# Layer norm, attention and routed experts on one core: a mask product per score group, a projection slot by slot, and an output stage cut into pieces of 14, 14 and 4 tiles

## The reference

```python
xn = layernorm(x)
qkv = xn @ W_qkv                       # 32 query heads, 16 key and value heads, of 64
scores = q k^T / 8 + slope[h] * (key position - query position), causal
s = (softmax(scores) v) @ W_out
# experts: 8, each 128 -> 512 -> 128 with gelu, two per token, weights from a softmax over the two
g = silu(experts(xn))
return x + s * g
```

## Time and profile before

| | |
|---|---|
| median of three executions | 1264.25 us |
| profiled execution | 1263.92 us |
| its span | 1262.0 us |
| TensorE busy | 1154.3 us, 91% of the span, 17610 products |
| VectorE busy | 1015.8 us, 80% |
| ScalarE busy | 935.5 us, 74% |
| GpSimd busy | 879.9 us, 70% |
| GpSimd, L743 (low parts) | 640 times 1038 ns |
| VectorE, L1348 (accumulation) | 64 times, mean 687 ns in the loops |
| TensorE, L881 (128 columns) | 1024 times, mean 219 ns |

### The profile page before, as it was taken

How to read it: one execution, slowest core, us unless ns; L and a number is a source line. 1 busy time by engine, 2 the same in 40 slices (tenths; PEclk the granted TensorE clock), 3 DMA queues, 4 the chain that set the end, 5 groups by cost and what they waited for, 6 DMA issues and landing times.

```text
span 1262.0 us, 54043 instructions
## 1 busy us (share of the span) xinstructions
PE 1154.3 (91%) x17610; PEld 915.0 (73%) x17610; DVE 1015.8 (80%) x3107; ACT 935.5 (74%) x1790; POOL 879.9 (70%) x1088
## 2 busy tenths in 40 slices
PE   1449999999999999998999789999999999999992
PEld 0327777777777777787888658777777777777782
DVE  8758888888888888885777668888888888888874
ACT  1328888888888888886666468888888888888882
POOL 9128888888888888884000068888888888888883
PEclk9669999999999999999999989999999999999996
DMA  6416666666666666674333366665555555555553
GB/s 211 171 38 134 142 140 148 143 142 144 144 142 144 144 142 144 145 141 93 86 89 82 99 156 137 136 137 133 133 133 133 133 133 133 133 133 133 133 116 84
DMA packets 286165, 165.10 MB, mean 131 GB/s; under 512 B 175011, under 2 KB 274691, under 8 KB 285445
## 3 DMA queue, kind: packets, MB, share of 16 engines
q1 hardware_dynamic: 281988, 155.63, 53.9%
q0 software_dynamic: 4096, 8.40, 2.3%
HBM read 15.76 MB, written 16.78 MB: 26 GB/s over the span
## 4 chain that ended last, share of the span: by engine, by line
PE 78%; DVE 6%; DMA 4%; issue 4%; ACT 3%; SPq 2%; POOL 2%; ACTq 0%; POOLq 0%; DVEq 0%
PE ps L880 10%; PE ps L854 10%; PE ps L782 8%; PE ps L783 7%; PE ps L784 7%; PE ps L884 6%; PE outs L911 6%; PE outs L915 5%; PE outs L913 5%; PE ps L881 4%; DMA k_st<-stage 3%; PE ps L887 2%; PE ps L863 2%; ACT q_st L1109 2%; PE outs L783 1%
## 5 line engine op out<-in xcount | busy, mean ns | idle before, releaser
L743 POOL TENSOR_TENSOR t_lo<-stage 128x512 f16<-128x512 f32 x640 | 654.6, 1038 | 106.6 <-ACT stage L1120 102.1
L1302 DVE CUSTOM_DVE_ANT_0 stage<-ps,kmask 128x512 bf16<-128x512 f32 (+3 forms) x1024 | 467.1, 488 | 118.8 <-PE ps L854 101.6
L1120 ACT ACTIVATE stage<-ps,slope 128x512 f32<-128x512 f32 (+1 forms) x768 | 455.6, 619 | 120.0 <-PE ps L887 82.1
L880 PE MATMUL ps<-q_st,k_st 128*128 128x256 f16 (+3 forms) x1024 | 305.8, 301 | 10.5 <-ACT stage L1120 6.9
L911 PE MATMUL outs<-v_sp,stage 128*128 128x65 f16 x2560 | 282.1, 194 | 4.3 <-DVE stage L1332 2.8
L913 PE MATMUL outs<-v_sp,stage 128*128 128x64 f16 x2560 | 281.9, 193 | 0.0
L915 PE MATMUL outs<-v_sp,t_lo 128*128 128x65 f16 x2560 | 281.8, 193 | 0.0
L854 PE MATMUL ps<-k_st,stage 128*128 128x512 f16 (+3 forms) x1024 | 251.7, 302 | 12.8 <-DVE spread L1302 5.5
L911 PEld LDWEIGHTS outs<-v_sp,stage 128*128 128x128 bf16 x2560 | 238.4, 98 | 12.2 <-issue 4.4
L913 PEld LDWEIGHTS outs<-v_sp,stage 128*128 128x128 bf16 x2560 | 235.9, 98 | 9.0 <-issue 0.3
L915 PEld LDWEIGHTS outs<-v_sp,t_lo 128*128 128x128 f16 x2560 | 235.9, 98 | 0.0
(11 more groups left out here) (199 smaller groups left out, 2731.6 us busy)
## 6 DMA issues: line engine op xcount, KB each, us to landing
k_st<-stage SPq DMA_DIRECT2D x256, 128.0 KB, 2.5
q_st<-stage SPq DMA_DIRECT2D x256, 128.0 KB, 2.4
q_st<-stage SPq DMA_DIRECT2D x256, 64.0 KB, 2.1
k_st<-stage SPq DMA_DIRECT2D x128, 64.0 KB, 2.1
slot_y<-stage SPq DMA_DIRECT2D x40, 128.0 KB, 2.0
X<-in_L_attn_inputs SPq DMA_DIRECT2D x8, 512.0 KB, 6.3
slot_x<-att SPq DMA_DIRECT2D x2, 2048.0 KB, 8.7
wx_raw<-in_L_ffn_w SPq DMA_DIRECT2D x64, 64.0 KB, 1.8
```

The lines of the kernel that those rows point to most:

```text
L743: pool.tensor_tensor(t_lo[r], t_p[r], upper(t_p[r]), ALU.subtract).then_inc(s[f"lo{u % NG}"], 1)
L880: pe.matmul(d, k[:, 0, at], q[:, 0, seen], start=True, stop=False, skip_group_check=True)
L1120: e = act.activation(t_p[r][:, c0:c1], S_ps[u % 2][:, c0:c1], ACT.Exp, scale=slope[:, bass.ds(pair_index(n) * 2 * SLOTS + sl * 2 + h, 1)])
L1302: ins = dve.tensor_tensor_reduce(junk[h][:, c0:c0 + w], M_ps[h][:, c0:c0 + w], kmask[:, SEQ - w:SEQ], -1.0 / 1024, 3e38, ALU.add, ALU.min, ...
```

## The change

1. `scores`: the mask product is made once per group, after all blocks, with an output in two pieces (67 columns in each block) where the group has two, and `late_q` read twice by a broadcast. The first product of the second block no longer has the start flag.
2. `project`: the wait for the bank comes first; then for each slot a wait for its transpose and the three products of all four token tiles.
3. `accumulate` multiplies by 1/WS, 64 times, in place of the factor in the output stage.
4. The output goes in pieces of 14, 14 and 4 tiles (1792, 1792 and 512 columns), a multiplication and an addition each: piece 0 on GpSimd, piece 1 on VectorE ahead of its last accumulation, piece 2 on VectorE after it. ScalarE applies Silu to pieces 0 and 1 ahead of the last cast of the last body (`out_hi` of body 63, slot 1), and to piece 2 after it. Pieces 0 and 1 wait for the accumulations of the first 56 bodies.

The expert stage is the same in both kernels.

```diff
+        LAST = NT - QT
+        PIECES = [(0, LAST // 2), (LAST // 2, LAST), (LAST, NT)]
+
         def out_chunk(v, c):
-            return v[:, 8 * c:8 * c + 8, :].rearrange("p t d -> p (t d)")
+            t0, t1 = PIECES[c]
+            return v[:, t0:t1, :].rearrange("p t d -> p (t d)")
+
+        def finish(eng, c):
+            need(eng, "silu", c + 1)
+            eng.wait_ge(s["acc"], BODIES if c == 2 else BODIES - PAIRS)
+            eng.wait_ge(s["xend"], 64)
+            a, g, xx = (out_chunk(v, c) for v in (att, mix, X))
+            eng.tensor_tensor(a, a, g, ALU.mult).then_inc(s[f"gated{c}"], 1)
+            eng.wait_ge(s[f"gated{c}"], 1)
+            eng.tensor_tensor(xx, xx, a, ALU.add).then_inc(s[f"fin{c}"], 1)
...
@@ sync
-            for c, name in ((0, "finP"), (2, "finD"), (1, "finP"), (3, "finD")):
-                sp.wait_ge(s[name], c % 2 + 1)
-                sp.dma_start(ot[:, 8 * c:8 * c + 8, :], X[:, 8 * c:8 * c + 8, :]).then_inc(s["outd"], 16)
+            for c, (t0, t1) in enumerate(PIECES):
+                sp.wait_ge(s[f"fin{c}"], 1)
+                sp.dma_start(ot[:, t0:t1, :], X[:, t0:t1, :]).then_inc(s["outd"], 16)
...
@@ gpsimd, after leave_bodies
-            pool.wait_ge(s["xend"], 64)
-            for c in range(2):
-                pool.wait_ge(s["gated"], c + 1)
-                xx = out_chunk(X, c)
-                pool.tensor_tensor(xx, xx, out_chunk(att, c), ALU.add).then_inc(s["finP"], 1)
+            finish(pool, 0)
...
@@ tensor, scores
-                    pe.matmul(d, k[:, 0, at], q[:, 0, seen], start=True, stop=False, skip_group_check=True)
+                    pe.matmul(d, k[:, 0, at], q[:, 0, seen], start=(c0 == 0), stop=False, skip_group_check=True)
...
-                    late = slice(0, P - LATE - 1)
-                    mm = pe.matmul(d[:, LATE:P], late_k[late, :], late_q[late, LATE:P],
-                                   start=False, stop=True, skip_group_check=True)
-                mm.then_inc(s[f"scored{u % NG}"], 1)
+                late, first = slice(0, P - LATE - 1), [c0 // P for _, _, c0 in GROUPS[u % NG]]
+                d = S_ps[u % 2].rearrange("p (t c) -> p t c", c=P)[:, first[0]:first[-1] + 1:max(first[-1], 1), LATE:P]
+                pe.matmul(d, late_k[late, :], late_q[late, LATE:P].unsqueeze(1).to_broadcast([P - LATE - 1, len(first), P - LATE]),
+                          start=False, stop=True, skip_group_check=True).then_inc(s[f"scored{u % NG}"], 1)
@@ tensor, project
+                bank_free(n, "O0")
                 for sl in range(SLOTS):
                     need(pe, f"ta{sl}", (n + 1) * 16)
-                bank_free(n, "O0")
-                for t in range(QT):
-                    tok = slice(t * P, (t + 1) * P)
-                    for sl in range(SLOTS):
-                        j = bass.ds(pair_index(n) * SLOTS + sl, 1)
+                    j = bass.ds(pair_index(n) * SLOTS + sl, 1)
+                    for t in range(QT):
+                        tok = slice(t * P, (t + 1) * P)
                         mm = three(bank_of("O0")[:, tok], aT[par][sl][:, tok],
...
-                                   start=(sl == 0), stop=(sl == SLOTS - 1))
+                                   start=(sl == 0 and t == 0), stop=(sl == SLOTS - 1), shared_bank=True)
                 mm.then_inc(s["op"], 1)
@@ scalar
+            def gates(c):
+                g = out_chunk(mix, c)
+                act.activation(g, g, ACT.Silu).then_inc(s["silu"], 1)
+
             def out_hi(n, _, sl):
+                final = isinstance(n, int) and (n, sl) == (BODIES - 1, 1)
+                if final:
+                    act.wait_ge(s["added"], NT)
+                    for c in range(2):
+                        gates(c)
                 act.wait_ge(s[f"nrm{sl}"], n + 1)
...
                 act.copy(by_head(a16[sl][:, 0:SEQ]), values_of(sl)).then_inc(s[f"ah{sl}"], 1)
+                if final:
+                    gates(2)
...
-            act.wait_ge(s["added"], NT)
-            act.activation(mix[:, :, :], mix[:, :, :], ACT.Silu).then_inc(s["silu"], 1)
@@ vector
             def accumulate(n, _par, _):
+                if isinstance(n, int) and n == BODIES - 1:
+                    finish(dve, 1)
                 dve.wait_ge(s["op"], n + 1)
...
-                dve.tensor_tensor(a, bank_of("O0")[:, :], a, ALU.add).then_inc(s["acc"], 1)
+                dve.scalar_tensor_tensor(out=a, in0=bank_of("O0")[:, :], scalar=1.0 / WS, in1=a, op0=ALU.mult,
+                                         op1=ALU.add).then_inc(s["acc"], 1)
...
-            dve.wait_ge(s["silu"], 1)
-            dve.wait_ge(s["acc"], BODIES)
-            dve.wait_ge(s["xend"], 64)
-            for c in range(4):
-                a, g, xx = (out_chunk(v, c) for v in (att, mix, X))
-                dve.scalar_tensor_tensor(out=a, in0=a, scalar=1.0 / WS, in1=g, op0=ALU.mult, op1=ALU.mult)\
-                   .then_inc(s["gated"], 1)
-                if c >= 2:
-                    dve.wait_ge(s["gated"], c + 1)
-                    dve.tensor_tensor(xx, xx, a, ALU.add).then_inc(s["finD"], 1)
+            finish(dve, 2)
```

More of the change, by code:

```diff
@@ L277, in build @@
             xload0 xload1 hmm0 hmm1 gelu0 gelu1 hhi hlo0 hlo1 ymm yout ystore0 ystore1
-            gated rd0 rd1 nrm0 nrm1 op acc ta0 ta1 ah0 ah1 al0 al1 rows
+            gated0 gated1 gated2 rd0 rd1 nrm0 nrm1 op acc ta0 ta1 ah0 ah1 al0 al1 rows
             turnc0 turnc1 crow0 crow1 copied
@@ L281, in build @@
             qmm0 qmm1 qh0 qh1 ql0 ql1 kmm kh kl vmm vh vl
-            finD finP outd""".split()
+            fin0 fin1 fin2 outd""".split()
         s = {n: sem("s_" + n) for n in names}
@@ L597, in _ @@
             ot = out.rearrange("b (t p) d -> p (b t) d", p=P)
-            for c, name in ((0, "finP"), (2, "finD"), (1, "finP"), (3, "finD")):
-                sp.wait_ge(s[name], c % 2 + 1)
-                sp.dma_start(ot[:, 8 * c:8 * c + 8, :], X[:, 8 * c:8 * c + 8, :]).then_inc(s["outd"], 16)
-            sp.wait_ge(s["outd"], 64)
+            for c, (t0, t1) in enumerate(PIECES):
+                sp.wait_ge(s[f"fin{c}"], 1)
+                sp.dma_start(ot[:, t0:t1, :], X[:, t0:t1, :]).then_inc(s["outd"], 16)
+            sp.wait_ge(s["outd"], 16 * len(PIECES))
         @block.gpsimd
```

## The result

Five executions of the changed kernel took 1253.48 to 1257.60 us, median **1255.62**, beside 1264.25 (1260.57 to 1268.05, five executions) for the kernel before: ratio 0.9931, 95% interval 0.9905 to 0.9957, so 8.6 us less, where 12.5 were forecast. Two later comparisons gave 0.9926 (0.9906 to 0.9945) and 0.9932 (0.9918 to 0.9946). The profiled execution took 1255.62 us.

What follows compares the result with a forecast made beforehand. The prediction took TensorE to pace both loops, but not the last 30 us. Mask product 2.8, projection 2.8 and the end 6.9 us summed to 12.5, from 1264.25 to 1251.7 us; range 1247.3 to 1257.3.

Steps and rivals of the forecast that it cites:

- signs that the prediction named for being wrong: Distances of 0.07 or more behind two-piece products, a gap at the thirteenth product, unchanged loop period, first store after 1241.
- The end: Output stage: Silu earlier, GpSimd's and VectorE's long instructions taking turns, stores without a gap; end at 1255.05 against 1262.0, 6.9 us.
- Projection in the last body: Last body: slot 0's half can run before slot 1's transpose lands; counted 0 because VectorE is busy until 1247.
- ScalarE's load without a drain: Output stage: the Silu table load costs 1.28 us, without the drain of about 1.38 us that the Trainium skill gives.
- Projection in the second loop: Slot 1's address stall on TensorE hidden, 0.11 us a body over 26 bodies: 2.8 us saved.
- Mask product: Score groups in both loops: 384 merges, each saving 0.008 us of TensorE, 3.1 us, of which 2.8 counted.
- The loops give nothing: Rival, both loops: another engine's wait replaces what TensorE saves, leaving only the end's 6.9 us: 1257.4; chance 0.10.
- The jam: Rival, output stage: VectorE gets two turns in a row, end 4.95 us early, loops give nothing: 1259.3; chance 0.07.
- the drain: Rival, ScalarE's switch to Silu: a drain makes everything at the end 1.4 us later: 1253.1; chance 0.05.
- the slow rival: Rival, mask product: two-piece output paid as its whole span, like 256 columns, 16.9 us more: 1271.5; chance 0.03.
- the race: Output stage: VectorE asks before GpSimd's product ends and goes next, by 0.4 us; rival "GpSimd first" 1249.8, chance 0.25.

Runs made afterwards that it cites:

- after_again: The changed kernel run once more with no edit: ratio 0.9926 (0.9906 to 0.9945) to the kernel before.
- tail_only: The changed kernel with the old `scores` and `project`, so only the new output stage and the accumulation's factor: ratio 0.9958 (0.9942 to 0.9975) to the kernel before.
- loops_only: The kernel before with the new `scores` and `project` and the old output stage: ratio 0.9972 (0.9960 to 0.9983).
- before_again: The kernel before run once more with no edit: ratio 1.0014 (1.0001 to 1.0027).
- project_only: The kernel before with only the projection done slot by slot: ratio 0.9982 (0.9969 to 0.9995).
- short_q: The changed kernel, each query projection's third product covering 256 columns instead of 512: 31.01 us a pair of bodies in the first loop, 31.29 in the second; one execution.
- merge_only: The kernel before with only the mask products merged to one per group: ratio 0.9981 (0.9967 to 0.9995).

## Why the prediction was right, and where its sizes were off

The direction, the parts and their order by size were right, and 1255.62 us lies between the ends given; it was 3.9 us short of the forecast of 1251.7. The end carries the result; of what was forecast for the loops about half came. Two of the signs that the prediction named for being wrong appeared: the first loop's period was unchanged, and the first store's data came at 1245.3, later than 1241. Everything up to the last exponential was to be 5.6 us earlier and was 1.1 us earlier. The long form of the expert stage isn't all of that: after_again has the short form, as has before, and its last exponential is only 1.9 us earlier (1230.93), with 0.9 us lost ahead of the first projection. By the prediction's own steps:

- **The end.** 6.9 us forecast. The time after it was right to 0.1 us (22.2), through the turns of the two engines, each step within half a microsecond: the first piece was ready at 1244.45, which is 1245.56 on the old clock (all was 1.11 us earlier), for the 1245.45 forecast. The subtrahend was one execution's 29.2; two other traces with the old output stage and the old projection have 28.6 and, with the merged mask product, 28.0. So the term is nearer 6.4; timed alone it gave 5.3 (3.2 to 7.3).
- **Projection in the last body: 0.** Right, shown by tail_only. In the old output stage it would have been worth 2.5 us, by the ends of loops_only and before_again.
- **ScalarE's load without a drain.** Right, in every trace with the new stage. The last cast was late by 0.68 us (1235.50 to 1236.18) for 0.15 forecast, and hidden as said.
- **Projection in the second loop: 2.8 us.** The stall went as forecast, 0.2 us a pair. In project_only the period is 0.12 shorter, 1.6 us over the 13 pairs, which is within the scatter of this loop.
- **Mask product: 2.8 us.** This is the step that failed, twice. The price: 134 columns cost 62 ns, not 58. I drew the line through the 256-column row; the 67-column row with 67 more columns at the 0.43 ns a column of that same line would have given an estimate of 33 + 29 = 62. That leaves 4 ns a merge, 1.5 us in all. And its premise: "TensorE paces the loops, so a column or a stall taken from it there is time". In the first loop it isn't so (short_q), and the period stayed at 31.06 to 31.13 us a pair through all edits of the change. What the merge gave in the first half lies ahead of the steady pairs (1.1 us, merge_only), where the prediction had nothing. The busy share of 99% that I rested it on counts durations of 0.19 us for products that follow at 0.03.
- **Both edits in the loops together.** Seven traces with both have 31.27 to 31.54 us a pair in the second loop (mean 31.48), three with neither 31.59 to 31.74 (mean 31.69): 0.21 x 13 = 2.7 us, for 5.6 in both loops forecast. With 6.4 at the end that is 9.1, and with the 1.1 of the early bodies 10.2. The three comparisons have 8.6 to 9.4, each with an interval of 2 to 3 us to either side, so the parts fit within it.
- **Rivals.** "The loops give nothing" was nearly half true. The jam, the drain and the slow rival didn't occur; the race went the forecast way in this kernel, at 0.77 us.

## What to carry to other kernels

A busy share of 99% on an engine whose instructions overlap doesn't show that it has no slack: look at the distances, and shorten one instruction without removing any to see whether the period follows. Where two engines exclude each other, a stage's end is found by laying their instructions end to end in the order in which they ask, and the first transfer's start, so the size of the first piece, is worth more than an even split. A profile of one execution can hold a stage's short or long form: take the subtrahend from two.

## What was not expected of the hardware

- A stage with the same code took 168.5 or 172.3 to 174.0 us, execution by execution, with the same order of instructions; the wait for one transposing load was 1.2 us in one and 4.0 in another.
- 60 products of 512 columns and 200 of 134 and 67, with 66 rows, back to back behind a stretch at the lower level, stayed at 1.2 GHz: TensorE was busy for 13.00 of 13 us at a granted clock of 0.50.
- A product with a hole in its output and one without differ by 1 ns at that level.
